# Gate and up products on split float32r operands, and three sets of attention buffers, in a transformer block with adaptive normalisation

## The reference

```python
h = layernorm(x) * (1 + ca) + sa
x = x + ga * attention(h)          # 16 heads of 16, causal, linear position bias, exact softmax
h = layernorm(x) * (1 + cb) + sb
xq = fp4_quant_dequant(h)          # blocks of 16 in a row, scale max/6, grid 0..6
h2 = silu(xq @ q(w_gate).T) * (xq @ q(w_up).T)      # 704 wide
x = x + gb * (fp4_quant_dequant(h2) @ q(w_down).T)
```

## Time and profile before

| | us |
|---|---|
| median of three runs | 3659.13 |
| lowest and highest | 3658.35, 3669.73 |
| the profiled execution | 3680.17 |
| its span, first to last instruction | 3678.4 |
| PE, DVE, ACT busy | 3400.2, 2859.7, 1862.1 |
| mean granted clock of PE | 0.944 |

### The profile page before, as it was taken

How to read it: one execution, slowest core, us unless ns; L and a number is a source line. 1 busy time by engine, 2 the same in 40 slices (tenths; PEclk the granted TensorE clock), 3 DMA queues, 4 the chain that set the end, 5 groups by cost and what they waited for, 6 DMA issues and landing times.

```text
span 3678.4 us, 62613 instructions
## 1 busy us (share of the span) xinstructions
PE 3400.2 (92%) x24952; PEld 1950.1 (53%) x24952; DVE 2859.7 (78%) x4538; ACT 1862.1 (51%) x2475; POOL 1082.0 (29%) x794
## 2 busy tenths in 40 slices
PE   6889999999999999999999999999999999999887
PEld 3345555555555555555555555555555555555455
DVE  7877869778786987868788786987868789687665
ACT  1555455555554555455555554655455555555441
POOL 2112324223242322324133142232323223241233
PEclk7889999999999999999998999999998999999898
DMA  8251413314323332423314323332423314332010
GB/s 152 55 81 28 76 40 68 65 28 77 56 53 60 52 70 39 79 44 61 65 32 72 56 50 63 51 68 42 79 48 56 66 33 71 57 50 54 16 32 12
DMA packets 134929, 207.65 MB, mean 56 GB/s; under 512 B 38848, under 2 KB 98832, under 8 KB 134640
## 3 DMA queue, kind: packets, MB, share of 16 engines
q1 hardware_dynamic: 134640, 203.66, 31.3%
HBM read 63.65 MB, written 17.89 MB: 22 GB/s over the span
## 4 chain that ended last, share of the span: by engine, by line
PE 71%; DVE 14%; ACT 10%; issue 2%; POOL 1%; DMA 1%; SPq 1%; ACTq 0%; POOLq 0%; DVEq 0%
PE banks L783 12%; PE banks L919 9%; PE banks L767 9%; ACT arena L982 8%; DVE top L1218 8%; PE banks L802 8%; PE banks L896 8%; PE banks L903 7%; PE banks L826 5%; PE banks L912 3%; PE banks L857 3%; PE banks L877 3%; PE banks L748 3%; ACT L982 2%; PE banks L887 1%
## 5 line engine op out<-in xcount | busy, mean ns | idle before, releaser
L1218 DVE TENSOR_REDUCE top<-banks 128x2 f32<-128x1024 f32 (+3 forms) x1280 | 1371.8, 1114 | 274.7 <-PE banks L748 171.4
L982 ACT ACTIVATE arena<-banks 128x1024 f32<-128x1024 f32 (+2 forms) x1280 | 1160.7, 940 | 784.4 <-PE banks L748 520.3
L802 PE MATMUL banks<-ka,qa 58*128 58x512 f32 (+3 forms) x3072 | 625.3, 442 | 130.1 <-ACT arena L982 94.2
L767 PE MATMUL banks<-qa,ka 60*128 60x512 f32 (+3 forms) x3072 | 590.9, 424 | 79.7 <-ACT arena L982 46.7
L783 PE MATMUL banks<-arena,va 128*17 128x512 f32 (+3 forms) x6144 | 641.1, 519 | 7.2 <-ACT arena L982 6.8
L767 PEld LDWEIGHTS banks<-qa,ka 60*128 60x128 f32 x3072 | 276.3, 192 | 407.2 <-ACT arena L982 175.2
L802 PEld LDWEIGHTS banks<-ka,qa 58*128 58x128 f32 x3072 | 291.1, 201 | 343.8 <-ACT arena L982 195.9
L1119 POOL TENSOR_TENSOR hid<-hid,tm 128x704 f32<-128x704 f32 x128 | 215.8, 1686 | 769.3 <-DVE hid L1196 769.3
L919 PE MATMUL banks<-wdT,hqT 128*128 128x256 f32 x1536 | 371.1, 392 | 3.4 <-ACT hqT L1024 3.4
L919 PEld LDWEIGHTS banks<-wdT,hqT 128*128 128x128 f32 x1536 | 290.1, 194 | 77.5 <-issue 23.1
L896 PE MATMUL banks<-wguT,xqT 128*128 128x352 f32 x1024 | 326.3, 462 | 0.7 <-ACT xqT L1015 0.7
(11 more groups left out here) (138 smaller groups left out, 4017.2 us busy)
## 6 DMA issues: line engine op xcount, KB each, us to landing
qa<-parts SPq DMA_DIRECT2D x384, 128.0 KB, 4.3
ka<-parts SPq DMA_DIRECT2D x384, 128.0 KB, 6.0
xa<-in_x SPq DMA_DIRECT2D x16, 1024.0 KB, 5.8
xr<-in_x SPq DMA_DIRECT2D x64, 256.0 KB, 3.0
out_x<-xr SPq DMA_DIRECT2D x64, 256.0 KB, 3.1
onT<-oT SPq DMA_DIRECT2D x252, 64.0 KB, 5.2
rsumT<-rsum_dram SPq DMA_DIRECT2D x63, 256.0 KB
ffn_rows<-rows_dram SPq DMA_DIRECT2D x16, 256.0 KB, 4.4
```

The source lines that it names most:

```text
L767: mm = pe.matmul(ps[:, at:at + w], ka[g][rows, pair, kt * P:(kt + 1) * P], qa[g][rows, pair, q0:q0 + w], start=m == 0, stop=s not in DIAGO ...
L802: mm = pe.matmul(ps[:, at:at + w], qa[g][rows, pair, qt * P:(qt + 1) * P], ka[g][rows, pair, c * BANK:c * BANK + w], start=m == 0, stop=no ...
L982: nc.scalar.activation(heads.rearrange("p (m r) q -> p r m q", r=2), scores, ACT.Exp).then_inc(a_free, 1)
L1218: nc.vector.tensor_reduce(tops, scores, AX.X, ALU.max).then_inc(d_free, 1)
```

## The change

Three things change in what is computed and where.

First, xqT and wguT become pairs of float32r tensors, high and low. ACT's copy writes the high part (a rounding), and a new step on DVE subtracts it from the transpose, which is still in PSUM: XL for activations, four per batch, and WL for weights, six in all. The bank is held until then. A gate or up product of float32 becomes three products of float32r: high x high, high x low weights, low x high weights. GA waits for XL.

Second, qa and ka are a ring of three sets, and group n of the run uses set n mod 3. This makes room for the pairs. MOVE waits for the last T of the group three earlier; since sets change their heads, the slope rows are written to DRAM once and come into qa with each MOVE of q, two more transfers. Twelve static copies stand at the start in the place of 16. The table for the conditioning's weights moves from wguT to featT.

Third, the planner has new costs and a new SHIFT table, and so all lists have another order. Lines moved by 20 to 40: XT is L917 in the new file, GA L928, UP L935, XL L1303, S L832, T L796, PV L812, masks L776, MOVE L654 and L659.

```diff
+LANDED = {"q": 32 * (len(Q_PARTS) + 1), "k": 32 * len(K_PARTS)}
...
+SETS = 3
...
+def earlier(b, g, n):
+
+    return divmod(b * NG + g - n, NG)
...
-    SHIFT = {"ACT CO": 62.0, "ACT GA": -91.0, "ACT HT": 37.0, "ACT LX": 48.0, "ACT T": 24.0, "ACT TR": -78.0, "ACT U": 13.0,
...
+    SHIFT = {"ACT CO": 29.0, "ACT GA": -113.0, "ACT HT": -32.0, "ACT LX": 8.0, "ACT T": 14.0, "ACT TR": -59.0,
...
+            p.add("SP", ("MOVE", b, u, g), 4.5 if UNITS[u][0] == "q" else 3.9, at + (g + 2) * L / NG, ("POOL", ("SPL", b, u)),
+                  ("PE", ("T", *earlier(b, g, SETS), NS - 1, jobs_of(NS - 1) - 1)), ("SP", ("TOP", *earlier(b, g, SETS - 1))),
+                  lag=6.0)
...
+               holder=("DVE", ("WL", 0, n)))
+            p.add("DVE", ("WL", 0, n), 0.69, 66.0 + 16.0 * n, ("ACT", ("WT", 0, n)))
...
+               ring="A", on="ACT", takes_cost=0.59, holder=("DVE", ("XL", b, r)))
+            p.add("DVE", ("XL", b, r), 0.69, due + 9, ("ACT", ("XT", b, r)))
...
-                    pe(("GA", b, t, k), 1.2, due + 10 + k, ("ACT", ("XT", b, r)), ("PE", ("HT", *tile(2 * r - 1), 1)),
+                    pe(("GA", b, t, k), 0.95, due + 10 + k, ("DVE", ("XL", b, r)), ("DVE", ("WL", 0, GU // 2)), ("PE", ("HT", *tile(2 * r - 1), 1)),
...
+LOW = {e: n for n, e in enumerate((e for e in PLAN.order["DVE"] if e[0] in ("WL", "XL")), 1)}
+WEIGHTS_LOW = max(LOW["WL", 0, n] for n in range(GU // 2 + 1))
...
-        qa = [sb(f"qa{g}", [P, PAIRS, S], F32R) for g in range(NG)]
-        ka = [sb(f"ka{g}", [P, PAIRS, S], F32R) for g in range(NG)]
+        qa = [sb(f"qa{n}", [P, PAIRS, S], F32R) for n in range(SETS)]
+        ka = [sb(f"ka{n}", [P, PAIRS, S], F32R) for n in range(SETS)]
...
-        xqT = [sb(f"xqT{n}", [P, C, 2 * P]) for n in range(2)]
+        xqT = [[sb(f"xqT{part}{n}", [P, C, 2 * P], F32R) for part in "hl"] for n in range(2)]
...
-        wguT = sb("wguT", [P, C, 2 * FF])
+        wguT = [sb(f"wguT{part}", [P, C, 2 * FF], F32R) for part in "hl"]
...
-        w_mod_sb = wguT[:, :, :].rearrange("p c n -> p (c n)")[:, 0:6 * D]
+        w_mod_sb = featT[:, :, :].rearrange("p c n -> p (c n)")[:, 0:6 * D]
...
+        def group_set(b, g):
+
+            n = (b * NG + g) % SETS
+            return qa[n], ka[n]
...
-            for g in range(NG):
+            for g in range(SETS):
...
             sp.wait_ge(slopes_ready, 1)
-            for g in range(NG):
-                for par in range(2):
-                    n = 2 * PAIRS * (2 * g + par)
-                    sp.dma_start(qa[g][HALF * par + SPLIT:HALF * par + KB, :, :].bitcast(F32),
-                                 slope_rows[n:n + 2 * PAIRS, :]).then_inc(static_rows, 16)
+            sp.dma_start(slope_dram, slope_rows).then_inc(slopes_out, 16)
+            sp.wait_ge(slopes_out, 16)
...
+                    qs, ks = group_set(b, g)
+                    dst, order = (qs, Q_PARTS) if name == "q" else (ks, K_PARTS)
                     sp.wait_ge(split_done, b * 4 + u + 1)
-                    if b:
-                        sp.wait_ge(a_full, in_a["T", b - 1, g, NS - 1, jobs_of(NS - 1) - 1])
+                    if b * NG + g >= SETS:
+                        sp.wait_ge(a_full, in_a["T", *earlier(b, g, SETS), NS - 1, jobs_of(NS - 1) - 1])
                     for par in range(2):
+                        if name == "q":
+                            n = 2 * PAIRS * (2 * g + par)
+                            sp.dma_start(dst[HALF * par + SPLIT:HALF * par + KB, :, :].bitcast(F32),
+                                         slope_dram[n:n + 2 * PAIRS, :]).then_inc(part_in[u, g], 16)
...
+                low = [LOW[o] for o in PLAN.before[e] if o in LOW]
+                if low:
+                    pe.wait_ge(low_done, max(low))
...
-                        src = xqT[(t // 2) % 2][:, :, (t % 2) * P:(t % 2 + 1) * P]
+                        high, low = (part[:, :, (t % 2) * P:(t % 2 + 1) * P] for part in xqT[(t // 2) % 2])
+                        terms = [(x[:, c, :], w[:, c, :]) for c in range(C) for x, w in ((high, wguT[0]), (high, wguT[1]), (low, wguT[0]))]
                         if kind == "GA":
                             ps = open_banks(e, a=[("XT", b, t // 2), ("WT", 0, GU // 2)])
-                            for c in range(C):
-                                mm = pe.matmul(ps[:, 0:FH], src[:, c, :], wguT[:, c, e[3] * FH:(e[3] + 1) * FH],
-                                               start=(c == 0), stop=(c == C - 1))
+                            pe.wait_ge(low_done, max(LOW["XL", b, t // 2], WEIGHTS_LOW))
+                            for n, (x, w) in enumerate(terms):
+                                mm = pe.matmul(ps[:, 0:FH], x, w[:, e[3] * FH:(e[3] + 1) * FH],
+                                               start=(n == 0), stop=(n == len(terms) - 1))
                             mm.then_inc(a_full, 1)
                         else:
                             ps = open_banks(e)
                             for k in range(2):
-                                for c in range(C):
-                                    mm = pe.matmul(ps[:, k * BANK:k * BANK + FH], src[:, c, :],
-                                                   wguT[:, c, FF + k * FH:FF + (k + 1) * FH],
-                                                   start=(c == 0), stop=(c == C - 1))
+                                for n, (x, w) in enumerate(terms):
+                                    mm = pe.matmul(ps[:, k * BANK:k * BANK + FH], x, w[:, FF + k * FH:FF + (k + 1) * FH],
+                                                   start=(n == 0), stop=(n == len(terms) - 1))
...
-                        nc.scalar.copy(wguT[:, :, 2 * n * P:(2 * n + tiles) * P],
+                        nc.scalar.copy(wguT[0][:, :, 2 * n * P:(2 * n + tiles) * P],
...
-                        nc.scalar.copy(xqT[e[2] % 2][:, :, :], ps[:, :].rearrange("p (c n) -> p c n", c=C)).then_inc(a_free, 1)
+                        nc.scalar.copy(xqT[e[2] % 2][0][:, :, :], ps[:, :].rearrange("p (c n) -> p c n", c=C)).then_inc(a_free, 1)
...
+                    elif kind == "WL":
+                        n = e[2]
+                        tiles = 2 if 2 * n + 1 < GU else 1
+                        at = slice(2 * n * P, (2 * n + tiles) * P)
+                        dve.wait_ge(a_free, in_a["WT", 0, n])
+                        nc.vector.tensor_tensor(wguT[1][:, :, at], bank(("WT", 0, n))[:, 0:C * tiles * P].rearrange("p (c n) -> p c n", c=C),
+                                                wguT[0][:, :, at].bitcast(F32), ALU.subtract).then_inc(low_done, 1)
+                    elif kind == "XL":
+                        r = e[2]
+                        high, low = xqT[r % 2]
+                        dve.wait_ge(a_free, in_a["XT", b, r])
+                        nc.vector.tensor_tensor(low[:, :, :], bank(("XT", b, r)).rearrange("p (c n) -> p c n", c=C),
+                                                high[:, :, :].bitcast(F32), ALU.subtract).then_inc(low_done, 1)
...
```

88 lines of the change are left out of this document (44 added, 44 removed), and 13 rows, old and new, of the table SHIFT.

## The result

The changed kernel takes 3617.45 us (median, 3611.33 to 3620.46), the kernel before 3662.67 us on the same chip. The ratio is 0.9873, 95% interval 0.985 to 0.9895. The gain is 45 us where 110 were forecast, and the time lies 2 us above the range. The profiled execution took 3620.46 us.

A forecast was written before the change was run, and what follows sets the result against it. PE was taken as the bound. Products -133, start -5, subtractions +6, waits +5 and half-clock spells +17 made -110 us on 3680; less 0.6% for plain runs, this gave 3549 us, range 3490 to 3615.

The forecast's parts named there:

- What bounds the kernel: PE (TensorE), busy for 92% of the span; time taken from it is worth nearly its own length.
- The product's price: Gate and up products: 150 ns per float32r instruction (upper bound 167), saving 146 us, 133 us of it on the path.
- XL: 64 subtractions on DVE for the activations' low part, 0.692 us each, 44 us of work, charged at +6 us.
- The start: Static and slope copies before the gate row: fewer of them, row about 5 us earlier, booked -5 us (-6 to +2).
- The ring at nothing: Three sets of q and k instead of four: enough slack for the moves, nothing booked.
- D: Rival: score groups wait for q and k moves behind the group three earlier, cancelling the gain; 3671 us, chance 0.05.
- The order at 0, bounds -30 and +30: PE's new order of gate, up and second-pair steps: no side clearly favoured, 0 us, bounds -30 and +30.
- What is given back: ACT and DVE in shorter batches: 5 us of waits, and a half-clock spell in every third batch, 17 us.
- B: Rival: gain half eaten by 167 ns instructions, one more half-clock spell per batch and exposed XL; about 3610 us, chance 0.20.
- A: Rival: gain arrives whole, half of PE's 141 us of waits for ACT goes, no spell added; about 3500 us, chance 0.20.
- C: Rival: float32r weight loads not hidden behind the product before, a tile takes 6.05 us; slower, about 3810 us, chance 0.05.

The follow-up runs named there:

- the faster order: Changed kernel with only other due times (SHIFT and the four projections' fractions), searched on a model: 3525.09 us, 0.9604 of the kernel before.
- the mixed table: Changed kernel with the old planner costs and SHIFT, but the new projection fractions and rule kept: 3905.74 us, 1.0639 of the kernel before.

## Why the prediction was wrong, step by step

- **What bounds the kernel** held: what PE no longer does came back nearly whole, 106 to 109 of 115 us. I had put 91% of it on the path; the runs give 92 to 95%, no difference within their intervals.
- **The product's price** was mis-sized: 160 ns, between the 150 that I took and my upper end of 167. The saving is 24 x 0.160 against 4.74 us, 0.90 us a tile and 115 us, not 146. The float32 row stood 3 ns over columns by clock, and I carried that over to the new kind of product; the pair in the attention scores, 17 ns over (230 for 213), was the nearer row. What the 13 ns over columns by clock (160 for 147) are is not shown. Together with the share on the path this term fell from 133 to 109 us. It is luck that this hardly moved the sum: I had taken 22 us off again as given back, for waits and a clock that the products did not bring, so they stood in it with 111.
- **XL** held: 683 ns for 692, PE waits 1.6 us in all for it, and without it the run is no shorter that could be measured.
- **The start**: the move of ka that the first score tile waits for lands at 48.91 + 7.24 = 56.15 us instead of 58.05, 2 us earlier, not 5. That the fill as a whole became 36 us shorter I did not see; 25 of them come with the order and the slope copies (468 for 493 us with float32 and four sets).
- **The ring at nothing**: probably 20 us, with PE waiting 26 us longer for DVE's row maxima and not for moves. The longest wait for a move is 8.0 us at the start, so D's mechanism did not occur.
- **The order at 0, bounds -30 and +30**: this is the step that failed. It cost 38 us in all, above the bound that I gave it, 3.2 us in each of the ten batches less the gain at the start, and another order of the same steps gains 92. Of the 64 us between the forecast of -110 and the -46 measured, 38 are this step and some 21 the ring, the low steps and the start (+22 where I had booked +1); the net of products and what is given back is 5 off. I had two fences of order before me and took an absence of a favoured side for a small effect.
- **What is given back**, 5 us of waits and one spell in every third batch, was a right observation with a wrong cause. Between before and after, idle time grew by 3.8 us and the loss at half level by (23.9 - 17.4) / 2 = 3.2 us per batch. That is 7.0 of the 7.2 us that the products free. But with float32 products in the same lists both are already there. The 2.1 us per batch that were gained are, but for 0.2, in PE's other busy time: without idle time and the loss at half level its work fell from 199.9 to 190.9 us, 9.0, and the 1.9 beyond the products come with the order alone (198.0). To which steps they belong I did not trace.
- **The rivals**: B gave nearly the time, 3610 us. Its spell per batch came (6.5 us more of half level in a batch, 3.2 us lost), but in the float32 kernel with the same lists as well, so the order brought it and not the emptier PE; the price went somewhat over half way from 150 to 167 ns; XL was not exposed. "Batches that shrink by less than 5 us" was seen, with a clock of 0.935 where B had under 0.93. No rival named the order as a loss of its own. A did not come with this order. Another one, at 3525 us, has what it named, in part: the two score lines wait 99 us for ACT where it was 141, and there are fewer spells.
- **C**, the exposed weight load, fell: every product of a tile loads its own 128 columns, at full height, and they follow each other at 160 ns. A load of 0.19 us stands in the trace beside the product ahead of it (the row below the list). The Trainium skill, page "TensorE: Matmul & The Clock Gate", Part 3, says that a load overlaps with products in flight only when the row groups differ; the measured spacing speaks against that, and agrees with Part 2 of the page, which lets a load go ahead into the background weight buffer.

The load of the product that starts at 1618.20 us, in order of time (start, length):

```profile
1618.05 0.19 PEld L928 LDWEIGHTS banks<-wguTh,xqTh 128*128 128x128 f32 x1
```

The sum as it came out, from the ratios one step apart: order +38 us (1.0103), ring and low steps +22 (to 1.0162), products -106 (to 0.9873), together -46. These are steps of one path; on another, in the faster order, the products bring 89.

## What to carry to other kernels

In a kernel whose engines each work a fixed list, a change of a step's length or of the number of buffers is two changes: the price of the steps, which can be read from rows, and a new order, which can't, and which was here worth from -92 us (a searched one) to +288 us (the mixed table) against the one that came with the change. Price the second by a bound as wide as orders of the same work have differed, or measure the new lists with the old work. When a fixed order leaves stretches with half-height products and waits alone, dense products of full height ahead of them are worth a try: at the one place compared here the level stayed full with them, and the order as a whole had 10 us less of half level in each batch. That the placement did it is not shown apart.

## What the runs showed of the hardware

- A float32r product of 128 x 352 at full height, with a new weight tile each, takes 160 ns from start to start, 13 more than 352 columns at 2.4 GHz; one of the two instructions of a float32 product takes 296.
- The granted level at half is no tax on a given amount of work: the same steps in two orders got it for 470 us (after) and for (1 - 0.951) x 2 x 3528 = 346 us of the run. In after it didn't follow the width of the stationary tile (0.934 with 32 columns, 0.935 with 17), and it rose to 690 us of the run, (1 - 0.903) x 2 x 3561, when two thirds of the gate and up products were left out.
